# A row's weight halves: loaded from DRAM by SyncE instead of copied and split per row, in a gated linear layer fused with a long convolution

## The chip, the cores and the metric

The kernel runs on one core of a Trainium2 chip. The metric is the time of the whole program on the device in microseconds; lower is better. In the text, PE is TensorE's matmul, PEld its weight load, DVE VectorE, ACT ScalarE, POOL GpSimd, SP SyncE. SPq and ACTq are what those engines' queues issue.

## What is computed

For 128 rows of the batch, `x` is [128, 128, 2048] in float32. The first layer picks one of sixteen 128 x 128 matrices per row and adds the product. The second is a masked long convolution along time with a kernel made from state space parameters.

```python
x = x + einsum('bct,bcd->bdt', x, weights[condition])      # one of 16 matrices per row b
u_m = x * mask                                             # mask: t < length[b]
kernel = 2 * real(einsum('hn,hnl->hl', Cs, exp(P)))        # one kernel of 2048 taps per channel h
y = irfft(rfft(u_m, 4096) * rfft(kernel, 4096))[..., :2048] + u_m * D
x = x + y * mask
```

## The kernel before

The identity is added to the sixteen weights once (`w_all`), so the first layer of a row is one matrix product. The time axis is cut into two segments of 1024 steps. The work has three parts.

**The row stage** takes the 128 rows of segment 0 and the first four of segment 1. SP loads a row (512 KB) into one of four `row_x` buffers, ACT copies the row's matrix out of `w_all` into `w_sel` (`pick_w`: a register load of the row's condition and one copy), PE multiplies in full float32, ACT copies the result out and issues its store to `x1_scratch`. DVE, POOL and ACT make the parameters of the convolution meanwhile (the set-up work), as "shares" put between groups of rows by `row_groups`.

**The interleaved stretch** works on one channel of segment 0 after another, with the batch on the partitions, and puts the remaining 124 rows of segment 1 between them: one row per channel. For a channel, SP loads the column `x1` of all rows into a `tile` (the trace calls it decay, for it lies in that buffer). PE transposes it (L877), ACT and DVE split it into two float32r parts (`u_hi`, `u_lo`). PE drives the states (`drive`), advances them chunk by chunk (`advance`, L929), and makes the output from the input (a Toeplitz matrix, `toep`, L937) and from the states. DVE takes the output under the mask (L801). Most products are three fast ones of high and low parts (`split_mm`, L895 to L897). POOL makes a decay matrix `e_mat` three or so channels ahead (`make_e`) from `par` (L463), which DVE's `mats` reads too (L757). The Toeplitz matrix goes through DRAM: DVE makes `k_pad` (L772), SP stores it (L329), and SP loads it skewed as `toep` (L337) once that store has landed; ACT makes `t_hi` (L623) and DVE `t_lo` (L784) of it.

**The row in a channel.** SP loads it three channels ahead (`load_row`, L307). In the channel before, ACT's `halve_w` loads the row's condition into a register (L539), copies the matrix to `w_sel` (L541) and to `w_hi` as float32r (L542), all of it between state 1 and the input's halves (`keep_u`); `halve_x` makes `x_hi` in two halves (L531), the second after state 3. POOL's `split_row` waits for it, makes `w_lo` (L488) and four pieces of `x_lo` (L491), and goes on to the next `par`. PE multiplies in `row_in_parts`, ACT takes the result to `row_y` (L548), SP stores it (L311).

**The order.** All orders are written out by hand, in one function `channels` per engine. SP's order in a channel is: Toeplitz load of the next channel, `x1` load of the one after, row load, store of k_pad (L329, waits for DVE), store of b_whole (L353, waits for ACT), store of the row's result, edge, output (L341, waits for DVE). Each engine goes through its own list in order, and a wait holds up all that is behind it.

**Segment 1** then runs the 128 channels again without rows.

## Time and profile before

| | |
|---|---|
| time, median of 3 runs | 2387.25 us (2386.72 to 2394.55) |
| the profiled execution: its time, its span | 2383.36 us, 2381.3 us |
| mean granted clock of TensorE | 0.991 |
| busy share of the span: PE, PEld, DVE, ACT, POOL | 93%, 81%, 84%, 69%, 56% |
| DMA, whole span | 648.07 MB, mean 272 GB/s |
| the interleaved stretch | about 424 to 1540 us |

Busy shares are means over parts with different limits; what a change in one part is worth is read from that part. PE's share is high because the ends of matmuls are modelled. A wait is listed by who waited, for whom, the total, how many times, and the longest. "issue" is time in which the engine waited for nothing that the profile shows; a register load falls under it.

### The profile page before, as it was taken

The page shows a single profiled execution, that of the slowest core. Times are in us where ns is not written, and L with a number is a line of the kernel's source. Part 1 is how long each engine was busy: PE and PEld are TensorE (multiplying, and loading weights), DVE is VectorE, ACT ScalarE, POOL GpSimd, SP SyncE. Part 2 cuts the span into 40 slices and gives each one's busy share as a digit, 9 for nine tenths or more (in the row PEclk, how much of TensorE's full clock was granted, in tenths as well). Part 3 has the DMA queues.
Part 4 walks back from the last instruction along what each step waited for, and adds up shares of the span by engine and source line. Part 5 has one row for each costly group of instructions (what it writes and reads, how often), then busy time and mean ns, then how long its engine had stood idle before and what let it go on. Part 6 is the DMA issues. An engine that isn't in the chain of part 4 may idle for free.

```text
span 2381.3 us, 61811 instructions
## 1 busy us (share of the span) xinstructions
PE 2225.9 (93%) x15101; PEld 1934.9 (81%) x15101; DVE 2007.1 (84%) x4125; ACT 1647.8 (69%) x4864; POOL 1322.1 (56%) x1864
## 2 busy tenths in 40 slices
PE   5777776999999999999999999999999999999999
PEld 1222222988888889988898888899999999999999
DVE  4999300999999899999999899988888888888887
ACT  4444544778777777777777777766766666766766
POOL 0894500777777777777777777634334334334332
PEclk9999999999999999999999999999999999999999
DMA  8999899788888888888888888767777777777776
GB/s 299 361 353 364 339 353 353 260 294 287 297 287 291 290 293 295 300 287 294 299 292 287 286 289 296 252 209 213 218 217 214 216 216 216 216 217 215 216 217 189
DMA packets 278052, 648.07 MB, mean 272 GB/s; under 512 B 31362, under 2 KB 146308, under 8 KB 278020
## 3 DMA queue, kind: packets, MB, share of 16 engines
q1 hardware_dynamic: 259012, 578.49, 75.1%
q10 hardware_dynamic: 19008, 69.21, 7.2%
q8 instruction: 13, 0.21, 0.0%
q14 instruction: 19, 0.16, 0.0%
HBM read 328.82 MB, written 318.77 MB: 272 GB/s over the span
## 4 chain that ended last, share of the span: by engine, by line
PE 40%; POOL 31%; issue 18%; ACTq 5%; ACT 3%; DMA 2%; POOLq 1%; DVE 1%; SPq 0%; DVEq 0%
POOL x_lo L491 13%; PE bank L895 7%; PE bank L896 7%; PE bank L897 7%; POOL outer L466 6%; PE bank L864 6%; PE bank L937 5%; PE bank L877 5%; POOL e_mat L471 4%; POOL e_rev L473 4%; ACTq L523 4%; PE bank L929 4%; POOL w_lo L488 2%; POOL par L463 1%; ACT w_sel L524 1%
## 5 line engine op out<-in xcount | busy, mean ns | idle before, releaser
L789 DVE TENSOR_TENSOR u_lo<-bank,u_hi 128x512 fp32r<-128x512 f32 x512 | 350.0, 684 | 98.2 <-ACT u_hi L602 98.1
L463 POOL COPY par<-table 128x72 f32 (+1 forms) x256 | 104.2, 407 | 552.5 <-PE bank L897 489.8
L491 POOL TENSOR_TENSOR x_lo<-row_x,x_hi 128x256 fp32r<-128x256 f32 x496 | 395.8, 828 | 0.0
L937 PE MATMUL bank<-toep,u_odd 128*128 128x128 f32 x2048 | 394.7, 274 | 0.0
L864 PE MATMUL bank<-row_x,w_sel 128*128 128x512 f32 x528 | 275.0, 648 | 124.9 <-ACT w_sel L524 109.5
L548 ACT ACTIVATE row_y<-bank 128x512 f32<-128x512 f32 x512 | 304.0, 594 | 116.9 <-PE bank L864 116.4
L801 DVE COPY_PREDICATED decay<-mask,bank 128x512 f32<-128x512 uint8 x512 | 375.3, 733 | 0.8 <-PE bank L897 0.6
L611 ACT ACTIVATE state<-bank 128x128 f32<-128x128 f32 x768 | 214.6, 279 | 221.1 <-PE bank L929 122.7
L895 PE MATMUL bank<-t_hi,u_hi 128*128 128x256 f32 x1024 | 354.5, 346 | 9.7 <-DVE decay L801 9.7
L864 PEld LDWEIGHTS bank<-row_x,w_sel 128*128 128x128 f32 x528 | 94.5, 199 | 302.8 <-issue 164.8
L466 POOL TENSOR_TENSOR outer<-par 128x256 f32<-128x256 f32 x512 | 317.5, 641 | 20.5
L937 PEld LDWEIGHTS bank<-toep,u_odd 128*128 128x128 f32 x2048 | 315.7, 190 | 0.0
L895 PE MATMUL bank<-e_hi,s_hi 128*128 128x256 f32 x896 | 307.8, 343 | 3.0 <-DVE s_lo L795 2.0
L602 ACT ACTIVATE u_hi<-bank 128x512 fp32r<-128x512 f32 x512 | 302.4, 591 | 0.0
L795 DVE TENSOR_TENSOR s_lo<-state,s_hi 128x128 fp32r<-128x128 f32 x768 | 251.2, 327 | 55.1 <-ACT s_hi L614 54.3
L897 PE MATMUL bank<-t_hi,u_lo 128*128 128x256 f32 x1024 | 288.5, 282 | 0.0
L896 PE MATMUL bank<-t_lo,u_hi 128*128 128x256 f32 x1024 | 286.9, 280 | 0.0
L877 PE MATMUL bank<-const,decay 128*128 128x128 f32 x2048 | 268.5, 274 | 8.6 <-DMA decay<-x_scratch 8.5
L929 PE MATMUL bank<-state,r_mat 128*128 128x128 f32 x1280 | 258.6, 284 | 0.0
L614 ACT ACTIVATE s_hi<-state 128x128 fp32r<-128x128 f32 x768 | 238.5, 311 | 24.3
L896 PE MATMUL bank<-e_lo,s_hi 128*128 128x256 f32 x896 | 252.8, 282 | 0.0
L897 PE MATMUL bank<-e_hi,s_lo 128*128 128x256 f32 x896 | 252.5, 282 | 0.0
(145 smaller groups left out, 5974.2 us busy)
## 6 DMA issues: line engine op xcount, KB each, us to landing
row_x<-in_x SPq DMA_DIRECT2D x256, 512.0 KB, 6.2
decay<-x_scratch SPq DMA_DIRECT2D x256, 512.0 KB, 5.6
out<-decay SPq DMA_DIRECT2D x256, 512.0 KB, 3.5
x_scratch<-row_y ACTq DMA_DIRECT2D x132, 512.0 KB, 5.9
x_scratch<-row_y SPq DMA_DIRECT2D x124, 512.0 KB, 3.6
toep<-k_scratch SPq DMA_DIRECT2D x256, 128.0 KB, 4.9
k_scratch<-k_pad SPq DMA_DIRECT2D x128, 192.0 KB, 4.8
b_scratch<-b_whole SPq DMA_DIRECT2D x128, 128.0 KB, 3.3
```

The source lines that it names most:

```text
L466: pool.tensor_tensor(outer[:, n, :].rearrange("p (a b) -> p a b", b=LOW), par[j][:, p0:p0 + LOW].unsqueeze(2).to_broadcast([P, LOW, LOW]), ...
L491: last = pool.tensor_tensor(x_lo[i][:, cols], row_x[j][:, cols], x_hi[i][:, cols].bitcast(fp32), ALU.subtract)
L548: nc.scalar.activation(row_y[j][:, q * BANK:(q + 1) * BANK], from_bank[:, :], ACT.Copy).then_inc(row_taken, 1)
L789: v.tensor_tensor(u_lo[j % 2][:, blocks, :], t_bank[q][:, :].rearrange("s (k b) -> s k b", b=B), u_hi[j % 2][:, blocks, :].bitcast(fp32), ...
L801: v.copy_predicated(tile[j][:, cols], mask[:, seg * SEG + q * BANK:seg * SEG + (q + 1) * BANK], y_bank[q][:, :]).then_inc(y_taken, 1)
L864: mm(to_bank[:, :], w_sel[j][:, :], row_x[j][:, q * BANK:(q + 1) * BANK], start=True, stop=True).then_inc(row_made, 1)
L877: ins = nc.tensor.transpose(t_bank[q][:, n * P:(n + 1) * P], tile[j][:, at:at + P], eye)
L895: mm(to, w_hi, m_hi, start=start, stop=False, skip_group_check=True)
L896: mm(to, w_hi, m_lo, start=False, stop=False, skip_group_check=True)
L897: return mm(to, w_lo, m_hi, start=False, stop=stop, skip_group_check=True)
L929: mm(s_bank[j % 2][:, c * P:(c + 1) * P], r_mat[j][:, :], whole[:, :], start=False, stop=True, skip_group_check=True).then_inc(s_made, 1)
L937: mm(y[:, P:CHUNK], u_odd[i][:, c, :], toep[j][:, 0:P], start=False, stop=True, skip_group_check=True)
```

## The change

After `w_all` is made, ACT and DVE split all sixteen matrices into high and low parts once, into `u_hi` and `u_lo`, which stand free in the row stage. SP stores them to a DRAM scratch `w_dram` in four DMAs. In the interleaved stretch SP loads the row's condition into a register and brings both parts with one DMA of 128 KB into `w_pair`, a buffer of four, right behind the row's load. ACT's register load and two copies and POOL's subtraction are gone. PE waits for the load before the row's first product.

```diff
--- before.py
+++ after.py
@@ -74,6 +74,7 @@
     x1_dram = [nc.dram_tensor(f"x1_scratch{i}", (B, H * SEG + PAD), fp32, kind="Internal").ap() for i in range(NSEG)]
     k_dram = nc.dram_tensor("k_scratch", (H, TOEP), fp32, kind="Internal").ap()
     b_dram = nc.dram_tensor("b_scratch", (H, P, 2 * P), fp32, kind="Internal").ap()
+    w_dram = nc.dram_tensor("w_scratch", (NCOND, P, 2, P), fp32, kind="Internal").ap()
     edge_dram = nc.dram_tensor("edge_scratch", (H, P, B), fp32, kind="Internal").ap()
 
     ctx = ExitStack()
@@ -156,8 +157,7 @@
         set_up.close()
         x_hi = [sb(f"x_hi{i}", [P, SEG], fp32r) for i in range(2)]
         x_lo = [sb(f"x_lo{i}", [P, SEG], fp32r) for i in range(2)]
-        w_hi = [sb(f"w_hi{i}", [P, P], fp32r) for i in range(2)]
-        w_lo = [sb(f"w_lo{i}", [P, P], fp32r) for i in range(2)]
+        w_pair = [sb(f"w_pair{i}", [P, 2, P], fp32r) for i in range(SLOTS)]
         b_whole = [sb(f"b_whole{i}", [P, 2, P]) for i in range(2)]
 
         bank = [ctx.enter_context(nc.psum_tensor(f"bank{i}", [P, BANK], fp32)) for i in range(8)]
@@ -172,6 +172,10 @@
         w_in = sem("w_in")
         w_ready = sem("w_ready")
         w_picked = sem("w_picked")
+        w_half = sem("w_half")
+        w_split = sem("w_split")
+        w_stored = sem("w_stored")
+        w_loaded = [sem(f"w_loaded{i}") for i in range(SLOTS)]
         x1_stored = [sem(f"x1_stored{i}") for i in range(SLOTS)]
         row_halved = sem("row_halved")
         row_split = sem("row_split")
@@ -310,6 +314,10 @@
                 sp.wait_ge(row_taken, n * NQ + NQ)
                 sp.dma_start(x1_dram[seg][bass.ds(b, 1), 0:H * SEG].rearrange("a (h t) -> (a h) t", t=SEG), row_y[j][:, :]).then_inc(x1_stored[j], 16)
 
+            def load_w(n, j):
+                which = sp.value_load(cond_sb[0:1, bass.ds(n, 1)], min_val=0, max_val=NCOND - 1)
+                sp.dma_start(w_pair[j][:, :, :].bitcast(fp32).rearrange("c a k -> c (a k)"), w_dram[bass.ds(which, 1), :, :, :].rearrange("w c a k -> (w c) (a k)")).then_inc(w_loaded[j], 16)
+
             def rows(g, seg):
                 for j in range(SLOTS):
                     n = g * SLOTS + j
@@ -362,6 +370,10 @@
             rows(0, 0)
             with sp.Fori(1, SETUP[-1] + 1) as g:
                 rows(g, 0)
+            sp.wait_ge(w_split, 2)
+            for i in range(2):
+                for n, half in enumerate((u_hi, u_lo)):
+                    sp.dma_start(w_dram[i * NBLK:(i + 1) * NBLK, :, n, :].rearrange("w c k -> c w k"), half[i][:, :, :].bitcast(fp32)).then_inc(w_stored, 16)
             sp.wait_ge(pads_zeroed, 2)
             for k in range(2):
                 store_kernel(k, k)
@@ -374,8 +386,10 @@
             sp.wait_ge(par_ready, 1)
             for k in range(2):
                 load_x1(0, k, k, 0)
+            sp.wait_ge(w_stored, 64)
             for n in range(ROWS_FIRST, ROWS_FIRST + 3):
                 load_row(n, n % SLOTS, 1, n - B)
+                load_w(n, n % SLOTS)
 
             def channels(g, seg, with_rows):
                 for j in range(SLOTS):
@@ -392,6 +406,7 @@
                         load_b(k + 3, j3)
                     if with_rows and not (isinstance(g, int) and k + 3 >= B - AHEAD):
                         load_row(k + ROWS_FIRST + 3, j3, 1, k + AHEAD + 3)
+                        load_w(k + ROWS_FIRST + 3, j3)
                     if then and then[0] == 0:
                         store_kernel(k + 2, j2)
                         store_b(k + 2, j2)
@@ -485,7 +500,6 @@
 
                 i = j % 2
                 pool.wait_ge(row_halved, m + 1)
-                pool.tensor_tensor(w_lo[i][:, :], w_sel[j][:, :], w_hi[i][:, :].bitcast(fp32), ALU.subtract)
                 for at in range(0, SEG, PIECE):
                     cols = slice(at, at + PIECE)
                     last = pool.tensor_tensor(x_lo[i][:, cols], row_x[j][:, cols], x_hi[i][:, cols].bitcast(fp32), ALU.subtract)
@@ -527,19 +541,17 @@
 
                 i, n, cols = j % 2, m + ROWS_FIRST, slice(q * BANK, (q + 1) * BANK)
                 if q == 0:
+                    act.wait_ge(row_made, n * NQ - NQ)
                     act.wait_ge(x_loaded[j], n * 4 + (16 - j * 4))
                 ins = nc.scalar.activation(x_hi[i][:, cols], row_x[j][:, cols], ACT.Copy)
                 if q == NQ - 1:
                     ins.then_inc(row_halved, 1)
 
-            def halve_w(m, j):
-
-                n = m + ROWS_FIRST
-                act.wait_ge(row_made, n * NQ - NQ)
-                which = act.value_load(cond_sb[0:1, bass.ds(n, 1)], min_val=0, max_val=NCOND - 1)
-                w = w_all[:, bass.ds(which, 1), :].rearrange("c k d -> c (k d)")
-                nc.scalar.activation(w_sel[j][:, :], w, ACT.Copy)
-                nc.scalar.activation(w_hi[j % 2][:, :], w, ACT.Copy)
+            def halve_weights():
+
+                act.wait_ge(w_ready, 1)
+                for i in range(2):
+                    nc.scalar.activation(u_hi[i][:, :, :], w_all[:, i * NBLK:(i + 1) * NBLK, :], ACT.Copy).then_inc(w_half, 1)
 
             def take_row(n, j, q, from_bank):
                 if q == 0 and not (isinstance(n, int) and n < SLOTS):
@@ -593,7 +605,7 @@
 
             act.wait_ge(consts_in, 16 * (NSETUP + 1))
             pick_w(0, 0)
-            row_groups(act, rows, base_sines, keep_parameters, lambda: make_sines(0), lambda: make_sines(1), lambda: first_matrices(0), lambda: first_matrices(1))
+            row_groups(act, rows, lambda: (halve_weights(), base_sines()), keep_parameters, lambda: make_sines(0), lambda: make_sines(1), lambda: first_matrices(0), lambda: first_matrices(1))
 
             def keep_u(k, j, q):
                 act.wait_ge(u_made, k * NQ + (q + 1))
@@ -622,10 +634,10 @@
                 act.wait_ge(toep_loaded[j], gd * 16 + 16)
                 nc.scalar.activation(t_hi[j][:, :], toep[j][:, :], ACT.Copy).then_inc(toep_half, 1)
 
+            act.wait_ge(w_stored, 64)
             for q in range(NQ):
                 keep_u(0, 0, q)
             halve_toeplitz(0, 0)
-            halve_w(0, 0)
             for q in range(NQ):
                 halve_x(0, 0, q)
 
@@ -639,7 +651,6 @@
                     next_row = with_rows and not (isinstance(g, int) and k + 1 >= B - AHEAD)
                     keep_s(seg, k, j, 1)
                     if next_row:
-                        halve_w(k + 1, j1)
                         halve_x(k + 1, j1, 0)
                     if after:
                         keep_u(k + 1, j1, 0)
@@ -739,6 +750,9 @@
             link(v.tensor_scalar(mask[:, :], step_i, len_f[:, 0:1], None, ALU.is_lt))
 
             dve.wait_ge(turned_kept, 1)
+            dve.wait_ge(w_half, 2)
+            for i in range(2):
+                v.tensor_tensor(u_lo[i][:, :, :], w_all[:, i * NBLK:(i + 1) * NBLK, :], u_hi[i][:, :, :].bitcast(fp32), ALU.subtract).then_inc(w_split, 1)
             for q in range(H // HS):
                 hs = slice(q * HS, (q + 1) * HS)
                 link(v.tensor_tensor(ex[0][:, :].rearrange("p (h k) -> p h k", k=NEXP), ar_t[:, hs].unsqueeze(2).to_broadcast([P, HS, NEXP]),
@@ -900,9 +914,10 @@
 
                 i, cols = j % 2, slice(q * BANK, (q + 1) * BANK)
                 if q == 0:
+                    pe.wait_ge(w_loaded[j], m * 4 + (16 - j * 4))
                     pe.wait_ge(row_split, m + 1)
                 pe.wait_ge(row_taken, m * NQ + (ROWS_FIRST * NQ + q))
-                split_mm(row_bank[:, :], w_hi[i][:, :], w_lo[i][:, :], x_hi[i][:, cols], x_lo[i][:, cols], start=True, stop=True).then_inc(row_made, 1)
+                split_mm(row_bank[:, :], w_pair[j][:, 0, :], w_pair[j][:, 1, :], x_hi[i][:, cols], x_lo[i][:, cols], start=True, stop=True).then_inc(row_made, 1)
 
             def drive(seg, k, j):
```

## Rows read from the trace of the kernel before

**Rows 1.** By stretch: length, busy PE, PEld, DVE, ACT, POOL; clock, DMA share, GB/s.

```profile
...
350.00:400.00 50.00, 35.09 (x74) 12.72 (x73) 2.67 (x7) 23.83 (x52) 3.03 (x5) 0.96 0.94 336
600.00:850.00 250.00, 245.26 (x1715) 221.42 (x1714) 229.09 (x471) 195.35 (x584) 185.05 (x279) 1.00 0.87 290
850.00:1290.00 440.00, 438.11 (x3067) 396.74 (x3066) 419.55 (x840) 342.56 (x1037) 328.19 (x493) 1.00 0.87 295
...
```

**Rows 2.** Line 329, SP's stores of k_pad: ns min/median/max, first and last start (three stretches).

```profile
...
L329 SPq DMA_DIRECT2D k_scratch<-k_pad x120: 343/356/371, 440.7 to 1510.2; - x120
...
L329 SPq DMA_DIRECT2D k_scratch<-k_pad x28: 355/356/356, 602.5 to 845.9; - x28
...
L329 SPq DMA_DIRECT2D k_scratch<-k_pad x49: 355/355/356, 855.1 to 1283.3; - x49
...
```

**Rows 3.** Waits in 850 to 1290 us: waiter <- releaser, us in total, times, longest.

```profile
...
POOL w_lo L488 <- ACT x_hi L531: 104.0, 49, 2.8
...
PEld bank L929 <- ACT state L611: 8.3, 26, 0.4
DVE r_tmp L757 <- POOL par L463: 7.9, 33, 0.3
DVE t_lo L784 <- ACT t_hi L623: 5.7, 17, 1.2
...
```

**Rows 4.** Waits in 600 to 850 us, same columns.

```profile
...
ACT t_hi L623 <- DMA toep<-k_scratch: 15.3, 18, 1.8
...
DVE r_tmp L757 <- POOL par L463: 3.5, 15, 0.2
...
PEld bank L929 <- ACT state L611: 2.4, 8, 0.4
...
```

**Rows 5.** Line 539, ScalarE's register load of a row's condition: ns min/median/max.

```profile
...
L539 ACTq FUSED_REGOPS  x240: 37/152/157, 412.3 to 1514.3; - x120
L539 ACTq TENSOR_LOAD <-cond_sb x124: 274/604/882, 412.0 to 1513.9; - x124
...
```

**Rows 6.** Groups of instructions in 850 to 1290 us: busy us, mean ns, idle before.

```profile
...
L541 ACT ACTIVATE w_sel<-w_all 128x128 f32 x50 | 15.5, 310 | 43.2 <-issue 43.2
...
L491 POOL TENSOR_TENSOR x_lo<-row_x,x_hi 128x256 fp32r<-128x256 f32 x196 | 157.9, 837 | 0.0
...
L488 POOL TENSOR_TENSOR w_lo<-w_sel,w_hi 128x128 fp32r<-128x128 f32 x49 | 23.7, 484 | 104.0 <-ACT x_hi L531 104.0
...
```

**Rows 7.** SP's own waits, first 850 to 1290 us, then 600 to 850 us.

```profile
...
SPq L329 <- DVE k_pad L772: 85.1, 49, 2.3
...
SPq L329 <- DVE k_pad L772: 40.5, 28, 2.4
...
SPq L337 <- DMA k_scratch<-k_pad: 8.5, 14, 1.6
...
```

**Rows 8.** DMA issues, median us to landing: 850 to 1290 us, then 600 to 850 us.

```profile
...
k_scratch<-k_pad SPq DMA_DIRECT2D x49, 192.0 KB, 4.5
...
k_scratch<-k_pad SPq DMA_DIRECT2D x28, 192.0 KB, 5.2
...
toep<-k_scratch SPq DMA_DIRECT2D x27, 128.0 KB, 4.4
...
```

**Rows 9.** Timeline of SP's queue at the start: start us, us, instruction.

```profile
...
8.05 3.14 SPq L307 DMA_DIRECT2D row_x<-in_x  x4
```

**Rows 10.** Set-up: the adding of the identity to the weights, their landing, one wait.

```profile
...
L679 DVE TENSOR_TENSOR w_all<-w_all,const x1: 2292/2292/2292, 9.0 to 9.0; 128x2048 f32<-128x2048 f32 x1
...
DMA to landing us min/median/max: 7.6/7.6/7.6
...
POOL table L448 <- ACT table L571: 49.5, 1, 49.5
...
```

**Rows 11.** Line 784 (t_lo on VectorE), 850 to 1290 us and 1600 to 2300 us: ns min/median/max.

```profile
...
L784 DVE TENSOR_TENSOR t_lo<-toep,t_hi x49: 425/851/970, 856.5 to 1284.3; 128x256 fp32r<-128x256 f32 x49
...
L784 DVE TENSOR_TENSOR t_lo<-toep,t_hi x110: 424/426/427, 1599.7 to 2294.3; 128x256 fp32r<-128x256 f32 x110
...
```

## The prediction

> **What bounds the kernel now.** I read the stretches first, then the waits, then SyncE's queue. The change acts in the interleaved stretch, where each of 124 channels carries one row of the first layer. SP's store of k_pad occurs once per channel, so its starts give the period: (1510.2 - 440.7)/119 = 8.99 us over all of them, (845.9 - 602.5)/27 = 9.01 in one part, (1283.3 - 855.1)/48 = 8.92 in a calmer one [rows 2]. The reader is to see that no engine alone is full. In the calm part DVE is busy 419.55 of 440 us, 8.51 us of each 8.92; the DMA engines are busy 87% of the time [rows 1]. PE looks full, but modelled matmul ends overstate it; its waits tell more.
>
> In the calm part the waits that recur are small and hang together. ACT halves a row, POOL then makes w_lo and four x_lo, and only then par of a later channel, for which DVE waits 7.9 us in 49 channels, 0.16 each. PE waits for ACT's copied state 8.3 us, 0.17 each; between state 1 and state 2 ACT does the weight's register load and two copies. DVE's wait on t_hi is 0.12 each [rows 3]. POOL's 104 us of waiting are slack, no cost. In the part with period 9.01 another wait stands out: ACT waits 15.3 us for the Toeplitz matrix from DRAM, while the par and state waits are 3.5 and 2.4 us in 28 channels [rows 4]. So there are two regimes: ACT, POOL and DVE coupled in one, and in the other the round trip k_pad, store, load, t_hi, t_lo.
>
> **What the change removes.** On ACT: the register load, whose idle time before w_sel is 43.2/50 = 0.86 us, w_sel 0.31 [rows 6], and w_hi, a like copy, so about 1.4 us of each channel, most of it before keep_u and the second state. On POOL: w_lo, 0.48 us [rows 6], which stands between the halved row and par. Both waits of the calm part (0.16 on DVE, 0.17 on PE) lose their cause. They lie partly over one another. The lower bound of the gain there is nothing, should a neighbour end just as late; the upper is 8.92 - 8.51 = 0.41, DVE without any idle time. I take 0.17, the size of either wait, over the 49 channels of the calm part: 8.3 us. Elsewhere the same waits are (3.5/28 = 0.12, 2.4/28 = 0.09) [rows 4]; I take 0.10 over the other 75: 7.5 us. Sum: 15.8 us less.
>
> **What it adds in the stretch.** On SP, per channel: a register load, 0.60 us in the median and 0.88 at most, the register operations behind it 0.15 [rows 5], and one more DMA issue of 0.36 [rows 2] with its address, about 1.3 us with gaps. It stands after the row load and before the store of k_pad. There SP now waits for DVE's k_pad: 85.1/49 = 1.74 us in the calm part, 40.5/28 = 1.45 elsewhere [rows 7]. So the SP work is hidden by that wait, just: cover left 0.1 to 0.4 us on average. Behind it are queued the stores of k_pad and b_whole, the row's store, the edge, the output, and then the next Toeplitz load. Were the cover gone, all of these would go out late by the excess.
>
> The weight itself is 128 KB per channel on queues that move 295 GB/s at a share of 0.87 [rows 1], so 339 GB/s when busy: 0.39 us of DMA time. It goes out just before k_pad's store and delays its landing by nothing (if the row load ahead is done) up to 0.39, or up to 3.14/4 = 0.79 us if issuing limits: four row loads in a row took that [rows 9]. I take 0.4. The DMA share rises from 0.87 to about (0.87 x 8.92 + 0.39)/8.8 = 0.93: still under full. k_pad's store lands 4.5 us after issue in the calm part, 5.2 elsewhere [rows 8]. SP waits for that landing before the Toeplitz load 8.5 us in 28 channels, 14 times [rows 7], so in half the channels the 0.4 reaches nobody, and in the calm part DVE seldom waits on this path at all. I cost it at nothing beyond what I took off the gain in the 75 channels; if that cover is gone it becomes the first rival. The w_pair load is issued three channels ahead, so PE's new wait ends long before; I cost it at 0.
>
> **What it adds in the set-up.** DVE subtracts two halves of 128 x 1024; the add of the identity over 2048 columns took 2.29 us [rows 10], so about 2.3 us, ACT as much. POOL later waited 49.5 us for ACT's second sine pass [rows 10], so DVE's line of set-up work is not what is late last; covered, and 2.3 us if not. Four stores of 512 KB, in pieces of 512 bytes, go out at about 360 us, where the DMA engines are 94% busy at 336 GB/s [rows 1] and rows follow as fast as they can be moved. 2.1 MB at 336 GB/s is 6.2 us. Below: nothing, if they fill the gap around the first matrices; above: w_all, half as many bytes in such pieces, landed 7.6 us after issue [rows 10], so 15 us. I take 6. The start of the stretch loses one weight copy and gains three register loads on SP; 0, with 2 us either way.
>
> **Sum.** -15.8 + 6 = -9.8 us, say -10, against the profiled execution's own 2383.4 us (span 2381.3): 2373.4. The median of the runs is 3.9 us above that execution, so 2377.
>
> **The rivals.**
> First, slower: the Toeplitz round trip takes over. From k_pad's end to t_lo there are SP's issue, the landing (5.2), the toep load (4.4) [rows 8] and t_hi. It spans a channel and a bit, and DVE's work from t_lo to the next-but-one k_pad fills the rest of two channels; so each 0.1 us in the trip costs half of that per channel once it binds. For it: the cover on SP is thin, and 15.3 us of waits on it exist already [rows 4]. Against it: in the calm part it hardly binds. With 0.4 us more in the trip it costs 0.20 x 75 = +15, the calm part gains nothing, set-up +6: +21, so 2408. It decides once k_pad's store lands more than some 0.4 us later than now in most channels. With the bound of 0.79 it is 0.39 x 75 = 29, +35 in all.
> Second, no difference: the calm part gains its 8.3 us, the rest nets nothing, the set-up takes 6: -2, 2385.
> Third, slower through the port. t_lo takes 0.851 us in the median beside POOL's work and 0.426 where POOL stands idle [rows 11]: something of POOL's holds DVE up. Without w_lo (0.48) the longer x_lo starts as t_hi ends, and t_lo could wait for its 0.84 [rows 6] instead: up to +0.35 a channel, 43 us, less the 15.8, plus 6: 2420; with half of that, 2399. It decides if t_lo's median rises over 1.0 us. The same sharing works the other way too: POOL works 0.48 us less per channel, and many of DVE's operations are lengthened by it. That is room below my 0.17, up to the 0.41 and a bit more.
> The Trainium skill speaks of this in "SBUF — State Buffer", section "Terms": the port pair that DVE and GpSimd share is locked for a whole instruction and the loser blocks fully. The doubled t_lo agrees with it; by that rule alone the sign of this change would hang on which POOL instruction holds the lock when t_hi ends, so the third rival is its forecast and gets its own chance.
>
> **How the numbers follow.** Forecast (faster, around 2377): 0.44. First rival 0.24. Third rival 0.07. Second rival 0.25. My measure for no change is 0.3%, 7 us. The best case, 0.41 less in all channels and set-up hidden, is 124 x 0.41 = 51, 2336; half the way there, with the lock relief, I take as the low end, 2350. The high end takes in the first rival with some of its bound: 2412. Likeliest case alone: 2360 to 2381. Faster 0.44, same 0.25, slower 0.31.
>
> **What would show it.** In the changed profile: the period of k_pad's stores falls to 8.75 in calm parts and 8.9 elsewhere; DVE's wait for par and PE's for the state are nearly gone; ACT goes from state 1 to the row's halving at once. SP's wait for k_pad falls from 1.45 or 1.74 to 0.1 to 0.4 us, not to zero. k_pad's landing reads 4.9 to 5.6. The stretch starts 6 us later. The prediction is wrong if the waits of t_hi for toep grow past their 15.3 us in 28 channels, if SP's register load takes over 1 us, or if t_lo gets longer.

## The result and the profile after

The changed kernel takes 2420.22 us in the median (2405.59 to 2423.66), the kernel before 2387.19 in the same comparison: ratio 1.0121, 95% interval 1.0082 to 1.0159. By the ratio it is slower by some 29 us, by the medians by 33, where 10 us less were forecast, and it lies above the stated range of 2350 to 2412. Runs more than 1.5% above the fastest of their kernel are left out of the ratios below: 4 of 12 of "register load alone", whose trace is of such a run, 3 of 12 of "no load, k_pad's store first" and 1 of 11 of "after, stores early". Its profiled execution took 2405.59 us, its span is 2403.7 us, 22.4 more than the span before.

The period first: SP's stores of k_pad, one per channel, over the whole stretch, then in the two parts of [rows 2].

```profile
...
L337 SPq DMA_DIRECT2D k_scratch<-k_pad x120: 343/356/1273, 431.9 to 1514.5; - x120
...
L337 SPq DMA_DIRECT2D k_scratch<-k_pad x27: 355/355/1273, 606.6 to 843.4; - x27
...
L337 SPq DMA_DIRECT2D k_scratch<-k_pad x49: 355/356/1017, 852.3 to 1288.4; - x49
...
```

The first line covers the stores of the stretch from its first one on. [rows 2] starts two channels later, so here are the same 120 stores of the kernel before:

```profile
...
L329 SPq DMA_DIRECT2D k_scratch<-k_pad x120: 343/356/371, 420.7 to 1492.7; - x120
...
```

Over the stretch the period is (1514.5 - 431.9)/119 = 9.10 us, against (1492.7 - 420.7)/119 = 9.01 (8.99 over the span of [rows 2]). In the former calm part it is (1288.4 - 852.3)/48 = 9.09 against 8.92, in the other (843.4 - 606.6)/26 = 9.11 against 9.01. The same 119 periods took 1082.6 us against 1072.0, 10.6 more. The first of these stores comes at 431.9 us against 420.7, so in these two traces all that lies ahead of the stretch takes 11.2 us more. With 0.6 us in the rest, that makes the 22.4 between the spans.

The waits in 850 to 1290 us (waiter, releaser, total, times, longest), where ACT's wait for the toep load was 3.6 us in 5 channels before, and the one in 600 to 850 us that answers to [rows 4].

```profile
...
POOL x_lo L505 <- ACT x_hi L546: 135.4, 49, 4.0
DVE t_lo L798 <- ACT t_hi L635: 50.5, 40, 2.6
ACT t_hi L635 <- DMA toep<-k_scratch: 40.5, 41, 2.6
...
PEld bank L909 <- DVE t_lo L798: 19.5, 14, 1.8
PE bank L909 <- DVE decay L815: 14.5, 16, 1.4
...
```

```profile
...
ACT t_hi L635 <- DMA toep<-k_scratch: 22.0, 25, 2.4
...
```

DVE's wait for par and PE's for the state have gone, as forecast. In their place ACT waits for the Toeplitz matrix from DRAM in 41 of 49 channels, 40.5 us in all, and behind it DVE 50.5 us (5.7 before) and PE 19.5 and 14.5. The reader is to see that the new wait costs more than the two that went. DVE's busy time fell too: 384.41 of 440 us against 419.55 [rows 1], so DVE has 55 us of idle time in this part where it had 20.

```profile
...
600.00:850.00 250.00, 240.38 (x1706) 218.23 (x1705) 219.30 (x467) 185.72 (x521) 169.70 (x250) 1.00 0.92 304
850.00:1290.00 440.00, 422.50 (x3006) 384.75 (x3005) 384.41 (x824) 326.92 (x918) 297.10 (x435) 1.00 0.91 302
...
```

SP's own waits in 850 to 1290 us, to set beside [rows 7]:

```profile
...
SPq L361 <- ACT b_hi L595: 70.2, 48, 2.8
SPq L345 <- DMA k_scratch<-k_pad: 28.9, 33, 2.2
...
SPq L337 <- DVE k_pad L786: 0.4, 2, 0.3
```

The wait for k_pad, 85.1 us in 49 channels, is gone (0.4): SP now comes to that store after DVE has made k_pad. The wait at L345, before the Toeplitz load, for the landing of that store appears in 33 of 49 channels (6.4 us in 15 before). One channel of SP's queue (start, length, instruction) shows the order:

```profile
...
1013.43 0.33 SPq L311 DMA_DIRECT2D row_x<-in_x  x1
1014.61 0.34 SPq L319 DMA_DIRECT2D w_pair<-w_scratch  x1
1015.20 1.02 SPq L337 DMA_DIRECT2D k_scratch<-k_pad  x1
1018.42 0.35 SPq L361 DMA_DIRECT2D b_scratch<-b_whole  x1
...
1020.99 0.33 SPq L349 DMA_DIRECT2D out<-decay  x1
1022.06 0.35 SPq L345 DMA_DIRECT2D toep<-k_scratch  x1
...
```

From the row's load to the store of k_pad 1.8 us pass, filled by the register load and the load of w_pair; the issue of the store itself is 1.02 us long here. The Toeplitz load leaves at 1022.06, behind the output's store at 1020.99. Landings in 850 to 1290 us, as in [rows 8]:

```profile
...
out<-decay SPq DMA_DIRECT2D x48, 512.0 KB, 4.3
k_scratch<-k_pad SPq DMA_DIRECT2D x49, 192.0 KB, 5.6
w_pair<-w_scratch SPq DMA_DIRECT2D x49, 128.0 KB, 5.6
...
toep<-k_scratch SPq DMA_DIRECT2D x48, 128.0 KB, 3.9
...
```

k_pad's store lands after 5.6 us (4.5 before). The register load on SP, and VectorE's t_lo as in [rows 11]:

```profile
...
L318 SPq TENSOR_LOAD <-cond_sb x124: 264/270/756, 418.2 to 1521.5; - x124
...
L798 DVE TENSOR_TENSOR t_lo<-toep,t_hi x48: 424/668/1024, 853.2 to 1280.8; 128x256 fp32r<-128x256 f32 x48
...
```

The register load takes 0.27 us on SP, less than the 0.60 on ACT [rows 5]. t_lo's median fell from 0.851 to 0.668 us.

The set-up: SP's queue around the four stores of the split weights, after and then before.

```profile
...
362.57 0.41 SPq L376 DMA_DIRECT2D w_scratch<-u_hi  x1
363.04 1.16 SPq L376 DMA_DIRECT2D w_scratch<-u_lo  x1
364.25 3.55 SPq L376 DMA_DIRECT2D w_scratch<-u_hi  x1
367.84 2.83 SPq L376 DMA_DIRECT2D w_scratch<-u_lo  x1
370.78 1.58 SPq L337 DMA_DIRECT2D k_scratch<-k_pad  x1
...
376.48 32.42 SPq L311 DMA_DIRECT2D row_x<-in_x  x12
...
```

```profile
...
358.62 0.36 SPq L329 DMA_DIRECT2D k_scratch<-k_pad  x1
...
363.24 32.83 SPq L307 DMA_DIRECT2D row_x<-in_x  x12
...
```

From SP's arrival there to the next row load 13.9 us pass, against 4.6 before. The third and fourth store hold SP for 3.55 and 2.83 us, and what stands behind them is slowed as well.

### The profile page after: what moved, and what is told of

It is laid out like the page before. It is cut to its first block, busy times and chain, and to the rows that moved or that the text cites. A ratio compares the mean times of both kernels' runs of the same rounds, so it can differ in the third digit from the quotient of the medians.

```text
span 2403.7 us, 61909 instructions
## 1 busy us (share of the span) xinstructions
PE 2200.4 (92%) x15101; PEld 1924.1 (80%) x15101; DVE 1954.5 (81%) x4127; ACT 1620.2 (67%) x4618; POOL 1263.8 (53%) x1740
## 4 chain that ended last, share of the span: by engine, by line
PE 49%; DMA 26%; SPq 8%; issue 7%; ACTq 5%; ACT 3%; DVE 2%; DVEq 0%
DMA k_scratch<-k_pad 16%; PE bank L909 9%; PE bank L911 9%; PE bank L910 9%; PE bank L891 6%; PE bank L952 6%; PE bank L878 6%; DMA toep<-k_scratch 5%; PE bank L944 4%; ACTq L537 4%; DMA decay<-x_scratch 3%; SPq L332 1%; SPq L318 1%; ACT row_y L560 1%; SPq L345 1%
## 5 line engine op out<-in xcount | busy, mean ns | idle before, releaser
L505 POOL TENSOR_TENSOR x_lo<-row_x,x_hi 128x256 fp32r<-128x256 f32 x496 | 382.6, 801 | 400.7 <-ACT x_hi L546 400.7
L878 PE MATMUL bank<-row_x,w_sel 128*128 128x512 f32 x528 | 268.2, 633 | 146.7 <-ACT w_sel L538 122.8
L481 POOL TENSOR_TENSOR outer<-par 128x256 f32<-128x256 f32 x512 | 325.4, 656 | 20.5
L809 DVE TENSOR_TENSOR s_lo<-state,s_hi 128x128 fp32r<-128x128 f32 x768 | 257.8, 336 | 58.0 <-ACT s_hi L626 57.1
L891 PEld LDWEIGHTS bank<-const,decay 128*128 128x128 f32 x2048 | 228.4, 141 | 29.8 <-issue 28.6
```

Of the source, the lines that this page charges most:

```text
L481: pool.tensor_tensor(outer[:, n, :].rearrange("p (a b) -> p a b", b=LOW), par[j][:, p0:p0 + LOW].unsqueeze(2).to_broadcast([P, LOW, LOW]), ...
L505: last = pool.tensor_tensor(x_lo[i][:, cols], row_x[j][:, cols], x_hi[i][:, cols].bitcast(fp32), ALU.subtract)
L878: mm(to_bank[:, :], w_sel[j][:, :], row_x[j][:, q * BANK:(q + 1) * BANK], start=True, stop=True).then_inc(row_made, 1)
L891: ins = nc.tensor.transpose(t_bank[q][:, n * P:(n + 1) * P], tile[j][:, at:at + P], eye)
```

## The experiments

All times are ratios to the kernel before, run on the same chip. The kernel before itself scattered there from about 2364 to 2398 us, far more than in its first runs, so beside the ratio I give the period from the trace, which scatters less: the four traces whose stretch is that of before have 8.96, 8.99, 9.01 and 9.02. The channels that the periods cover differ by a few at either end; over the stores of channels 4 to 123 in every trace they shift by at most 0.02 us (after 9.08, before 8.99). ACT's wait for toep scatters more, from 15.2 to 30.0 us in those four. "Toep wait" is ACT's wait for the Toeplitz load in 600 to 1400 us, with the number of channels of some 90; "landing" is that of k_pad's store.

| kernel | ratio (95%) | period, us | toep wait | landing |
|---|---|---|---|---|
| before | 1 | 8.99 | 24.7, 28 | 4.8 |
| before, second trace | | 9.02 | 30.0, 38 | 5.1 |
| after | 1.0121 (1.0082 to 1.0159) | 9.10 | 70.8, 74 | 5.6 |
| set-up alone | 1.0097 (1.0064 to 1.0130) | 8.96 | 15.2, 23 | 4.9 |
| set-up without its stores | 1.0042 (1.0013 to 1.0071) | 9.01 | 23.5, 31 | 4.7 |
| no load of w_pair | 1.0045 (1.0018 to 1.0072) | 8.94 | 52.8, 55 | 5.5 |
| register load alone | 0.9986 (0.9951 to 1.0020) | 8.91 | 57.2, 69 | 5.3 |
| DMA alone | 1.0134 (1.0093 to 1.0175) | 9.11 | 66.3, 67 | 6.0 |
| load of w_pair twice | 1.0230 (1.0198 to 1.0262) | 9.40 | 82.0, 80 | 5.6 |
| before, k_pad's store first | 1.0037 (1.0010 to 1.0064) | 9.03 | 31.5, 55 | 3.0 |
| no load, k_pad's store first | 1.0006 (0.9970 to 1.0042) | 8.88 | 66.2, 75 | 3.6 |
| after, k_pad's store first | 1.0057 (1.0023 to 1.0092) | 9.05 | 84.6, 76 | 4.2 |
| before, both moves | 0.9989 (0.9960 to 1.0017) | 8.98 | none listed | 2.8 |
| no load, both moves | 0.9887 (0.9860 to 0.9915) | 8.63 | none listed | 3.1 |
| after, both moves | 0.9914 (0.9883 to 0.9945) | 8.71 | 10.4, 28 | 3.8 |
| after, stores early | 1.0096 (1.0062 to 1.0130) | 9.15 | 77.1, 75 | 5.7 |
| after, both moves, stores early | 0.9876 (0.9842 to 0.9911) | 8.71 | 4.9, 13 | 3.8 |

**First round: the change in its parts.** The set-up alone keeps the stretch as it was before and only splits and stores the weights. The cut shows the difference from the changed kernel in part.

```diff
-            def load_w(n, j):
-                ...
-                split_mm(row_bank[:, :], w_pair[j][:, 0, :], w_pair[j][:, 1, :], ...
+                split_mm(row_bank[:, :], w_hi[i][:, :], w_lo[i][:, :], ...
```

> The set-up of the change alone (sixteen weights split once and stored to DRAM, never loaded), the interleaved stretch as before. Theory A, the set-up's stores hold up SP's row loads: the first store of k_pad of the stretch, at 420.7 us before and 431.9 after the change, comes at 431 to 432 and the time is 11 us more than before, some 2398. Theory B, the later start comes from the start of the stretch (three register loads and three more loads on SP): start within 3 us of before's, time within 3 us of 2387. The prediction had 6 us for this part.

The ratio is 1.0097, 23 us in this comparison, with the stretch's period at 8.96. So the set-up costs more than the 11 us that the two first traces show apart. In its trace the stretch starts at 438.3 us, and SP needs 15.2 us around the stores (13.9 in the changed kernel). The cost is there without any register load at the stretch's start, which speaks for theory A as to the kind; its size was missed by both.

The relief alone: the four buffers are filled once, ahead of the stretch, and never again, so the rows of segment 1 are multiplied with the wrong weights, here and in every kernel below that lacks this load, its register load or its address.

```diff
-                        load_w(k + ROWS_FIRST + 3, j3)
-                    pe.wait_ge(w_loaded[j], m * 4 + (16 - j * 4))
+                    pe.wait_ge(w_loaded[j], 16)
```

> The change without the load of w_pair in the stretch: the four buffers are filled once and used for all rows, so the second segment's rows get the wrong weights; ACT's and POOL's work is gone as in the change, SP and DMA have nothing more to do than before. Theory A, the relief of ACT and POOL is worth what was predicted (16 us) or more and the load costs it: period of k_pad's stores 8.6 to 8.85 us, time 2387 + 11 - 16 to - 40, 2358 to 2382. Theory B, the relief is worth nothing since another engine is as late: period 8.95 to 9.0, time 2396 to 2400.

The period is (1514.3 - 433.1)/121 = 8.94. ACT and POOL have all of their relief, SP and the queues carry nothing new, and 0.05 us a channel is all that comes of it, 6 us in all, no more than the scatter of the period. The ratio of 1.0045 is above 1 because this kernel pays for the set-up too. The waits in 600 to 1400 us, SP's wait for k_pad and the landing of its store:

```profile
...
DVE t_lo L798 <- ACT t_hi L635: 58.3, 60, 2.8
...
ACT t_hi L635 <- DMA toep<-k_scratch: 52.8, 55, 2.4
...
SPq L337 <- DVE k_pad L786: 94.8, 89, 2.1
...
k_scratch<-k_pad SPq DMA_DIRECT2D x90, 192.0 KB, 5.5
...
```

The wait for toep has doubled (24.7 before), though nothing was added to the queues. The engines come to t_hi sooner and the matrix is not there. Theory B nearly in its number, but not in its reason: no engine is as late, a transfer is. The store of k_pad lands after 5.5 us, against 4.8 to 5.1 in the two traces of before, with no load of w_pair on the queues at all: it now goes out 1.5 us behind the row's load of 512 KB in the median, where it was 2.1.

The register load without the DMA, and the DMA without the register load (from a fixed address):

```diff
-                        load_w(k + ROWS_FIRST + 3, j3)
+                        sp.value_load(cond_sb[0:1, bass.ds(k + ROWS_FIRST + 3, 1)], min_val=0, max_val=NCOND - 1)
```

> As the kernel without the load of w_pair, but SP does the register load of the condition at the place where the change has it (its result is not used, the weights are wrong as there). Theory A, the register load (0.27 us and some 0.2 of register operations in the trace after) is covered by SP's wait for k_pad: within 4 us of the kernel without any load. Theory B, the register load takes SP's cover: 10 us or more above it, and SP's wait for k_pad, 1.5 us before, falls under 0.5.

```diff
-                        load_w(k + ROWS_FIRST + 3, j3)
+                        sp.dma_start(w_pair[j3][:, :, :]..., w_dram[j3:j3 + 1, :, :, :]...).then_inc(w_loaded[j3], 16)
```

> The change with the DMA of 128 KB at its place but from a fixed address, without the register load (the rows of the second segment get the wrong weights). Theory A, what costs is the DMA ahead of k_pad's store: k_pad's store lands 5.4 to 5.6 us after issue as in the change and the time is at least 2405. Theory B, it is SP's time, register load and issue together: landing as here but the time falls by a third to a half of the way to the kernel without a load, 2385 to 2400.

With the register load alone the period is 8.91, no worse than without any load (this kernel's times scatter from 2357 to 2402 us, so I go by the period and not by its ratio). SP's wait for k_pad fell to 36.1 us in 72 of some 90 channels, 0.40 us a channel, so the load took most of the cover that was left, as theory B said, and yet cost nothing, as theory A said. With the DMA alone it is 9.11, all of the changed kernel's 9.10, the landing at 6.0 us. The DMA costs some 0.19 us a channel (9.10 and 9.11 against 8.91 and 8.94) and the register load nothing that these traces can show.

**Second round: is it the round trip of k_pad?** My theory then was the prediction's first rival: the store of k_pad lands too late for the Toeplitz load. The store was put ahead of the row's load, in before, in the kernel without the load, and in the changed kernel.

```diff
                     if then:
                         load_x1(then[0], then[1], j2, then[2])
                     ...
+                    if then and then[0] == 0:
+                        store_kernel(k + 2, j2)
                     if with_rows and not (isinstance(g, int) and k + 3 >= B - AHEAD):
                         load_row(k + ROWS_FIRST + 3, j3, 1, k + AHEAD + 3)
                         load_w(k + ROWS_FIRST + 3, j3)
                     if then and then[0] == 0:
-                        store_kernel(k + 2, j2)
                         store_b(k + 2, j2)
```

> The kernel before with one edit in SP's order of a channel: the store of k_pad goes out ahead of the row's load of 512 KB instead of behind it. Theory A, the round trip of the Toeplitz matrix (store of k_pad, landing, load) is one of the two things that set the period: the store lands 3.5 to 4.2 us after issue instead of 4.8, ACT's wait for toep (24.7 us in 28 channels over 800 us) falls under 10, period 8.85 to 8.93 against 8.99, time down 8 to 17 us. Theory B, before the change the round trip had slack: same waits elsewhere, time within 5 us.

> The kernel without the load of w_pair in the stretch (weights of the second segment's rows wrong), with the store of k_pad ahead of the row's load. Theory A, ACT's and POOL's relief was eaten by the Toeplitz round trip: the wait for toep (52.8 us in 55 channels) falls under 20 and the period from 8.95 to 8.6 to 8.75, time 25 to 40 us under the kernel without the load. Theory B, the relief itself is worth little because DVE or PE is as late: period 8.85 or more.

> The changed kernel with the store of k_pad ahead of the row's load and of the load of w_pair. Theory A, the weight's load costs because it stands before k_pad's store on SP and on the queues: SP waits for k_pad again, landing 3.6 to 4.4 us, period 8.6 to 8.85 against 9.09, time 25 to 55 us under the changed kernel. Theory B, the 16 MB more on the DMA queues are the cost wherever they go: period 9.0 or more.

That theory fell. Of the kernel before with this edit, the toep wait, the store's landing and the Toeplitz load's own landing, in 600 to 1400 us:

```profile
...
ACT t_hi L624 <- DMA toep<-k_scratch: 31.5, 55, 2.2
...
k_scratch<-k_pad SPq DMA_DIRECT2D x89, 192.0 KB, 3.0
...
toep<-k_scratch SPq DMA_DIRECT2D x89, 128.0 KB, 4.3
...
```

The landing fell to 3.0 us and SP never waited for it, yet the toep wait did not fall (31.5 us, against 15.2 to 30.0 in the four traces without this edit) and the kernel was if anything slower (1.0037). Without the load the period became 8.88, with it 9.05: a little, nowhere near 8.75. In numbers both came out as theory B had it. Of the changed kernel with this edit, 600 to 1400 us:

```profile
...
ACT t_hi L636 <- DMA toep<-k_scratch: 84.6, 76, 3.0
...
SPq L345 <- DMA k_scratch<-k_pad: 0.3, 1, 0.3
...
toep<-k_scratch SPq DMA_DIRECT2D x89, 128.0 KB, 4.5
...
```

SP's wait for the landing, 61.0 us in 66 channels of the changed kernel, is gone, but the Toeplitz load that follows takes 4.5 us to land instead of 3.8, and ACT waits no less for it than in the changed kernel (84.6 us against 70.8). What stayed is the last leg: the Toeplitz load is issued behind the output's store of 512 KB, which waits for the end of a channel, takes about 4 us to land, and is wanted some 4 us into the next channel.

The last run of this round takes the four stores out of the set-up alone and leaves the splitting.

```diff
-            for i in range(2):
-                for n, half in enumerate((u_hi, u_lo)):
-                    sp.dma_start(w_dram[i * NBLK:(i + 1) * NBLK, :, n, :]..., half[i]...).then_inc(w_stored, 16)
```

> The set-up alone without its four stores: ACT and DVE split the sixteen weights, nothing is stored or loaded, the stretch as before. Theory A, the stores make the set-up's cost (ratio 1.0097 with them): ratio 0.999 to 1.002. Theory B, half of it or more is the splitting on ACT and DVE, which holds up the row stage: ratio 1.004 to 1.008.

The ratio of 1.0042 is one of theory B, but its interval reaches from 1.0013 to 1.0071. The splitting may cost something and the stores something; the intervals of 1.0042 and 1.0097 overlap slightly.

**Third round: the Toeplitz load ahead of the output's store.** With k_pad's store early it can go out two channels ahead, before the output's store; one more Toeplitz load stands ahead of the stretch for it. This move without the early store was not run, so all that follows is of both moves together.

```diff
-                    if after and after[0] == 0:
-                        load_toeplitz(0, k + 1, j1, after[2])
                     ...
+                    if then and then[0] == 0:
+                        load_toeplitz(0, k + 2, j2, then[2])
                     store_x2(seg, k, j)
```

> As the last kernel without the load of w_pair (k_pad's store ahead of the row's load; weights wrong), and the Toeplitz load of a channel goes out a channel's end earlier: ahead of the store of the output of 512 KB instead of behind it. Theory A, the wait for toep (66.2 us in 75 channels of 800 us) is what ate ACT's and POOL's relief: it falls under 15 us and the period from 8.88 to 8.6 to 8.75. Theory B, DVE or PE would be as late: the wait falls but the period stays above 8.83.

Without the load the period is (1498.3 - 445.4)/122 = 8.63. Two waits, and the stretch 600 to 1400 us (length, busy PE, PEld, DVE, ACT, POOL, clock, DMA share, GB/s):

```profile
...
ACT state L625 <- PE bank L913: 111.6, 93, 1.6
...
DVE t_lo L800 <- ACT t_hi L637: 2.5, 9, 0.3
...
600.00:1400.00 800.00, 799.41 (x5748) 736.38 (x5747) 789.92 (x1576) 615.06 (x1763) 577.50 (x835) 1.00 0.91 304
...
```

DVE is busy 789.92 of 800 us: now an engine is the bound, and this is what the relief was worth all along, 0.35 us a channel against the 8.98 that before has with both moves, 43 us over 124 channels. Between the two ratios (0.9887 and 0.9989) lie only 24 us; the kernel without the load has also paid for the set-up.

> The changed kernel with both moves on SP: k_pad's store ahead of the row's load, the Toeplitz load ahead of the output's store. Theory A, as there: period 8.6 to 8.8 against 9.09, time 35 to 60 us under the changed kernel, at or under the kernel before. Theory B, the DMA engines, at 92% with the load of w_pair, are the limit: landings all grow, period 8.95 or more.

The changed kernel with both moves has a period of 8.71 and a ratio of 0.9914; it beats both kernels.

```profile
...
ACT t_hi L637 <- DMA toep<-k_scratch: 10.4, 28, 0.7
...
q1 hardware_dynamic: 118969, 252.96, 93.9%
...
toep<-k_scratch SPq DMA_DIRECT2D x92, 128.0 KB, 4.7
...
```

The DMA engines are busy 93.9% of the time, more than in the changed kernel, and the Toeplitz load takes 4.7 us to land. That no longer matters much, for it leaves earlier: 4.8 us before t_hi starts in the median, against 3.9 in the changed kernel. So the 16 MB more are not what held the changed kernel at 9.10, and the load costs 0.08 us a channel here (8.71 against 8.63) where it cost 0.19. The second round's theory B, that they cost the same wherever they go, falls with this.

> The kernel before with the same two moves on SP. Theory A: the waits of DVE for par and of PE for the state stay and the wait for toep goes, period 8.88 to 8.93 against 8.99 (the calm part of its trace has 8.92), time down 6 to 14 us. Theory B, no difference: within 5 us.

```profile
...
PEld bank L931 <- ACT state L613: 28.7, 75, 0.6
DVE r_tmp L759 <- POOL par L465: 18.2, 72, 0.3
...
```

In the kernel before the same moves do nothing (8.98, ratio 0.9989). The toep wait is gone, and the waits for par and for the state are there in full. This is the mirror of the kernel without the load: taken away alone, the one bound is worth 0.01 us and the other 0.05, which the scatter of the period covers; both together are worth 0.35.

Last in this round, the weight's load is issued twice.

```diff
+                sp.dma_start(w_all[:, 2 * j:2 * j + 2, :]..., w_dram[bass.ds(which, 1), :, :, :]...).then_inc(w_loaded[j], 16)
                 sp.dma_start(w_pair[j][:, :, :]..., w_dram[bass.ds(which, 1), :, :, :]...).then_inc(w_loaded[j], 16)
```

> The changed kernel with the weight's load of 128 KB issued twice per row (the second copy goes to w_all, which nothing reads then). Theory A, the DMA queues ahead of k_pad's store and the Toeplitz load are the cost: the one load costs 0.19 us a channel (9.09 to 9.11 against 8.91 to 8.94), a second at least as much, period 9.25 to 9.5, time 20 to 50 us over the changed kernel. Theory B, one load fills a gap that existed and the cost is in its being there at all: period within 0.05 of 9.1.

The second 128 KB cost 0.30 us more a channel (9.40). The toep wait and the queues' share in 600 to 1400 us:

```profile
...
ACT t_hi L637 <- DMA toep<-k_scratch: 82.0, 80, 3.0
...
q1 hardware_dynamic: 123048, 246.46, 95.4%
...
```

**Fourth round: the place of the set-up's stores.** They go out after group 19 of the row stage, where ACT's sine passes stop the rows for a while.

```diff
-            with sp.Fori(1, SETUP[-1] + 1) as g:
+            with sp.Fori(1, 20) as g:
                 rows(g, 0)
             sp.wait_ge(w_split, 2)
             ...
+            with sp.Fori(20, SETUP[-1] + 1) as g:
+                rows(g, 0)
```

> The changed kernel, with nothing but the set-up's four stores moved to after group 19. Theory A as there: 5 to 12 us under the changed kernel (ratio 1.0121 there), 1.007 to 1.010, the stretch's period unchanged at 9.09 to 9.11. Theory B, place doesn't matter: 1.011 to 1.014.

> The version with both moves on SP (ratio 0.9914), with the set-up's four stores of the split weights issued after group 19 of the row stage instead of after group 29, where ACT's sine passes leave the DMA engines at 78%. Theory A, the stores cost 10 us or so where they block SP ahead of the first k_pad stores, and fill a gap here: 5 to 12 us less than that version, ratio 0.986 to 0.989. Theory B, their place doesn't matter: ratio 0.990 to 0.993.

> The kernel before once more, for a second trace. The first k_pad store of the stretch came at 420.7 us in the first trace, and between 422.3 and 439.4 in the kernels run so far, whatever their set-up. Theory A, the row stage varies from run to run by this much: it comes at up to 438 here, and the stretch's period is 8.97 to 9.02. Theory B, the changed set-up makes the late starts: 418 to 423.

Both ratios are lower than those of the kernels they were made from, 1.0096 against 1.0121 and 0.9876 against 0.9914, but the intervals overlap, so a gain of some 6 to 9 us is likely and not shown. The period of "after, stores early" was to stay at 9.09 to 9.11 and is 9.15; the difference is within the 0.06 by which the four traces of one stretch differ. The last kernel is the fastest that I ran: 2353.6 us in the median beside 2382.3 for the kernel before. The second trace of before starts its stretch at 419.2 us, like the first, but two other kernels with the same set-up start theirs at 408.9 and 426.3 (before with both moves, and with k_pad's store first). The time at which SP has issued the first 30 groups' rows scatters all the same, whatever the set-up: 352.6, 358.5, 358.6 and 369.9 us where it is that of before, 352.4 to 380.0 where the weights are split. I can't take a cost of the splitting out of that.

## Why the prediction was wrong

**What bounds the kernel.** The two regimes were read rightly. The mistake was to price each as if the other stood aside. Against the sum's -15.8 in the stretch and +6 for the set-up, the two traces show +10.6 and +11.2.

**The gain, 15.8 us: this step failed.** The waits for par and state did go. That both waits of the calm part "lose their cause" held; "I take 0.17, the size of either wait, over the 49 channels" did not. The relief alone was worth 6 us at most, since the Toeplitz load came as late as before and the engines reached it sooner. The slack on this load was thin: in the trace before, the median time from its landing to the start of t_hi is 0.46 us in 850 to 1290 us and 0.02 in 600 to 850; without the load of w_pair it is 0.02 in both: the relief used it up. What the prediction left out is this wait for toep in the price of the gain; the runs with both moves on SP show it, for there the relief is worth 0.35 us a channel, twice the 0.17 that was forecast. I had looked at waits, which show nothing of a transfer that arrives just in time.

**SP's time hidden by the wait for k_pad.** The forecast was "cover left 0.1 to 0.4 us on average": nothing was left (0.4 us in 49 channels). Part of the cover went to the relief already, 94.8 us of wait in 89 channels without any load against 143.9 in the same part before. The register load itself was 0.27 us and hidden, as the run with it alone shows; it never took over 1 us (0.76 at most).

**The weight's DMA, costed at nothing.** This step failed too: it costs some 0.19 us a channel, 24 us. The landing of 4.9 to 5.6 was forecast and came as 5.6, but this was luck: without any load it is 5.5 already, because the store moved closer behind the row's load. "In half the channels the 0.4 reaches nobody" failed: in 600 to 1400 us SP waited for the landing in 66 of 88 channels (35 of 89 before), and ACT for toep in 74.

**The first rival** named the right loop, and its size was near: +15 in the stretch against 10.6 between the traces, +21 in all against 22.4 between the spans, 29 by the ratio. The nearness is part luck. It let the calm part gain nothing and the rest lose 0.20 us a channel; measured, the calm part lost most, 0.17 us (8.92 to 9.09), and the rest 0.10 (9.01 to 9.11). And the store's landing is not the link that decides. SP does wait for it in the changed kernel, but with that wait removed the period only fell to 9.05. What brought the period down to 8.71 was to put the Toeplitz load ahead of the output's store as well.

**The third rival** gave 2420, the measured time, and that is an accident: t_lo's median fell to 0.668 us where it had to rise above 1.0. Its mechanism is real all the same. In the trace before, 600 to 1400 us, t_lo took 0.49 us in the median where it started beside w_lo (30 times) and 0.95 beside x_lo (59 times). One of them, and t_lo in 600 to 1400 us with both moves, first in the kernel before, then without the load:

```profile
...
1007.34 0.61 POOL L488 TENSOR_TENSOR w_lo<-w_sel,w_hi 128x128 fp32r<-128x128 f32 x1 [2.12 <-ACT x_hi L531]
...
1007.60 0.63 DVE L784 TENSOR_TENSOR t_lo<-toep,t_hi 128x256 fp32r<-128x256 f32 x1
...
```

```profile
...
L786 DVE TENSOR_TENSOR t_lo<-toep,t_hi x89: 478/637/966, 607.7 to 1397.9; 128x256 fp32r<-128x256 f32 x89
...
L800 DVE TENSOR_TENSOR t_lo<-toep,t_hi x93: 759/951/961, 601.8 to 1396.0; 128x256 fp32r<-128x256 f32 x93
...
```

t_lo ends at 1008.23, 0.28 us after w_lo's end at 1007.95, and so does every one of the 89 t_lo of 600 to 1400 us in the kernel before, and of the 88 in the changed kernel: 0.28 us after the end of an instruction of POOL. So its length goes by what POOL has left to do when it starts, 0.56 us in the median before and 0.35 in the changed kernel. It became shorter there because it starts at another point of x_lo, not because w_lo is gone. With both moves and without w_lo it always starts beside x_lo with 0.67 us left, and the two rows show 0.951 us against 0.637. So without w_lo DVE loses 0.2 to 0.3 us a channel at this place (mean and median), and the 8.63 has that in it. By the rule of the Trainium skill ("SBUF — State Buffer", "Terms") the loser is blocked while the other holds the pair; these ends, 0.28 us after POOL's, agree with it.

**The set-up, 6 us: sized too low.** The traces give 9.3 us for the stores' block (13.9 against 4.6) and 11.2 in all, the ratio of the set-up alone 23 us (15 to 31). The term was sized by bytes. The rows behind the stores were held by SP, which stood still at their issue; I had costed no such time. Over all traces, the ten kernels that split the weights and store them after group 29 start their stretch at 422.3 to 442.4 us, 432.0 in the mean, and the four with the set-up of before at 408.9 to 426.3, 418.8 in the mean: 13 us, twice the forecast. What fills the gap to 23 us stays open; the row stage scatters by more than 10 us from run to run.

## What to carry over

A wait that a profile shows can be taken away for nothing if a transfer now arrives just in time; before pricing the gain, read for each DMA how long after its landing it is used, and ask which one is late next. Two bounds of nearly the same height must be taken away together: here each alone was worth at most 0.05 us a channel, both 0.35. In an in-order queue of DMAs, put the small one that an engine waits for ahead of the large ones that are not wanted so soon; the two moves together were worth 4% of the period with the load added.

## What the runs showed of the hardware

The register load took 0.27 us in the median on SP and 0.60 on ACT. A store of 512 KB in pieces of 512 bytes held SP at its issue for 3.55 and 2.83 us as third and fourth in a row (0.41 and 1.16 for the first two), against a median of 0.36 us for the stores of k_pad. The DMA engines reached a share of 93.9% in the changed kernel with both moves, and its period of 8.71 us was shorter than in all kernels with one load of w_pair per row and the old order (9.10 to 9.15 at 90.6 to 92.1%). t_lo on VectorE ended 0.28 us after the GpSimd instruction that it ran beside, in all 177 cases of two traces, and took 0.951 us in the median where it always began beside x_lo, against 0.426 us beside an idle GpSimd [rows 11].
